# A selective scan in pairs: one scan instruction over two units, with ScalarE writing the restart of the second

## The reference, cut to what matters

```
x_dbl = einsum('bkdl,kcd->bkcl', xs, x_proj_weight)      # dt (6), B (16), C (16)
delta = softplus(dt_proj(dt) + bias)                     # 96 channels
h     = exp(delta * A) * h + (delta * u) * B             # 16 states for each channel, over l
y     = sum over the states of h * C, + D * u
```

## Time and profile before

| What | us |
|---|---|
| median of 3 runs | 5436.18 |
| lowest, highest | 5427.06, 5442.36 |
| span of the profiled execution | 5432.0 |
| VectorE busy in it | 4515.3 |
| GpSimd busy | 4129.8 |
| TensorE busy | 4644.7 |
| ScalarE busy | 2890.6 |

### The profile page before, as it was taken

How to read it: one execution, slowest core, us unless ns; L and a number is a source line. 1 busy time by engine, 2 the same in 40 slices (tenths; PEclk the granted TensorE clock), 3 DMA queues, 4 the chain that set the end, 5 groups by cost and what they waited for, 6 DMA issues and landing times. The chain is left out here.

```text
span 5432.0 us, 72922 instructions
## 1 busy us (share of the span) xinstructions
PE 4644.7 (86%) x15210; PEld 2119.9 (39%) x15210; DVE 4515.3 (83%) x4928; ACT 2890.6 (53%) x4502; POOL 4129.8 (76%) x2854
## 2 busy tenths in 40 slices
PE   7998887956999999963978888888888888888887
PEld 2332554623666666642522222222222222222222
DVE  4776445452599999997969999999999999999996
ACT  6885555621111111111357767777777777777776
POOL 2454545532589898987869999999999999999993
PEclk9998999978999999986989999999999999999998
DMA  2000101067677777744057667666776776677773
GB/s 52 1 1 14 56 22 51 27 191 208 130 146 146 143 146 142 149 85 99 0 142 188 185 186 189 184 185 189 187 189 179 188 189 187 181 188 188 187 186 94
DMA packets 385402, 733.35 MB, mean 135 GB/s; under 512 B 77948, under 2 KB 119080, under 8 KB 370920
## 3 DMA queue, kind: packets, MB, share of 16 engines
q1 hardware_dynamic: 385128, 730.30, 54.8%
HBM read 594.31 MB, written 82.32 MB: 125 GB/s over the span
## 5 line engine op out<-in xcount | busy, mean ns | idle before, releaser
L2194 POOL TENSOR_TENSOR l_hc<-l_h,l_c_rep 128x512 f32<-128x512 f32 x1536 | 1927.8, 1273 | 211.3 <-DVE l_h L2248 181.1
L2248 DVE TENSOR_TENSOR_SCAN l_h<-l_p_da,l_h,l_bu 128x512 f32<-128x512 f32 x1120 | 1403.4, 1269 | 5.0 <-ACT l_p_da L2099 2.5
L2099 ACT ACTIVATE l_p_da<-l_p_da,l_a_neg 128x512 f32<-128x512 f32 x1536 | 1008.1, 657 | 729.3 <-PE l_p_da L1954 713.1
L1400 POOL TENSOR_TENSOR l2b_prod<-l2b_v,l2b_attn 128x1568 f32<-128x1568 f32 x276 | 937.3, 3449 | 232.1 <-ACT l2b_attn L1361 116.7
L1954 PE MATMUL l_p_da<-l_stacked,l_pick 96*128 96x512 f32 x1536 | 908.4, 593 | 190.3 <-DVE l_h L2248 180.5
L2233 DVE TENSOR_TENSOR l_bu<-l_du_rep,l_p_b 128x512 f32<-128x512 f32 x1280 | 840.8, 657 | 27.9 <-DMA l_du_rep<-du_scratch 22.2
L1954 PEld LDWEIGHTS l_p_da<-l_stacked,l_pick 96*128 96x128 f32 x1536 | 293.2, 192 | 1161.0 <-DVE l_h L2248 896.8
L1448 DVE TENSOR_REDUCE l2b_osum<-l2b_prod 128x32 f32<-128x1568 f32 x384 | 665.7, 1780 | 63.0 <-POOL l2b_prod L1400 59.3
L1962 PE MATMUL l_p_y<-l_hc,l_y_pick 128*32 128x512 f32 x3072 | 562.9, 626 | 71.8 <-POOL l_hc L2194 71.7
L1353 ACT ACTIVATE l2b_logits<-l2b_conv,l2b_this_b 98x512 f32<-98x512 f32 x96 | 66.2, 689 | 861.5 <-PE l2b_conv L1318 861.5
L1318 PE MATMUL l2b_conv<-l2b_img_high,l2b_w_conv_high 128*98 128x512 f32 x1344 | 356.2, 418 | 32.2 <-DMA l2b_img_low<-qkv_scratch 32.2
(11 more groups left out here) (261 smaller groups left out, 8495.8 us busy)
## 6 DMA issues: line engine op xcount, KB each, us to landing
l_du_rep<-du_scratch SPq DMA_DIRECT2D x1536, 256.0 KB, 3.8
l2b_img_high<-qkv_scratch SPq DMA_DIRECT2D x192, 306.2 KB, 5.7
l2b_img_low<-qkv_scratch SPq DMA_DIRECT2D x192, 306.2 KB, 9.5
l_stacked<-l_parts SPq DMA_DIRECT2D x512, 96.0 KB, 2.7
l2b_v<-v_scratch SPq DMA_DIRECT2D x192, 152.0 KB, 6.5
qkv_scratch<-l2a_strip SPq DMA_DIRECT2D x32, 840.0 KB, 5.2
du_scratch<-l_du SPq DMA_DIRECT2D x128, 192.0 KB, 2.1
l_w_raw<-L_w_sed SPq DMA_DIRECT2D x32, 576.0 KB, 3.7
```

The source lines that it names most:

```text
L1400: return eng.tensor_tensor(dst.rearrange("q x (dy dx) -> q x dy dx", dx=WIN), window, attn_half[:, :, unit % 2].rearrange("q x (dy dx) -> ...
L2099: act.activation(p_da[i % DAS][:], p_da[i % DAS][:], ACT.Exp, scale=a_neg[:, k * G + GRP[i]:k * G + GRP[i] + 1]).then_inc(s_da, 1)
L2194: pool.tensor_tensor(hc[:, (G * par + i) % HCS, :], h[:, i, :], c_rep[:, par, :], ALU.mult).then_inc(s_hc, 1)
L2248: dve.tensor_tensor_scan(h[:, i, way], p_da[i % DAS][:, way], of, state, ALU.mult, ALU.add).then_inc(s_h, 1)
```

## The change

The 12 units become 6 pairs. One scan instruction now covers two units, 128x1024, over one flat row of 1024 columns. For the second unit to begin afresh, its decay in the first column is set to 0 and its own beginning, old decay x last h + bu, is written into `bu`. ScalarE does this (`decays`): it saves the exponential of that column (`joint_da`), does the two exponentials of 511 and 512 columns, writes the 0 into PSUM and writes the new `bu` column, with scale and bias from columns. Backward directions scan the flat row from its end, so there it is unit 0 of the pair that is restarted. `p_da` is now two pairs of banks, and `p_y` one bank for two.

The products by B and by C are made in pairs too: VectorE has four B pairs (0, 1, 3, 4), GpSimd two (2, 5), where VectorE had ten units and GpSimd two. du is made by VectorE, straight from the PSUM bank. `kept` is gone; delta's constant comes in by a 97th row of the operands. SyncE stores du ahead of the restack. TensorE, ScalarE and GpSimd have new orders.

```diff
             def decays(n, k, c, p):
+                act.wait_ge(s_rep, G * n + 2 * p + 1)
+                act.activation(joint_da[:, p % 2:p % 2 + 1], da[:, e, at:at + 1], ACT.Exp, scale=rate(2 * p + e)).then_inc(s_join, 1)
+                act.activation(da[:, e, rest], da[:, e, rest], ACT.Exp, scale=rate(2 * p + e))
+                act.wait_ge(s_rep, G * n + 2 * p + 2)
+                act.activation(da[:, 1 - e, :], da[:, 1 - e, :], ACT.Exp, scale=rate(2 * p + 1 - e))
+                act.wait_ge(s_join, PAIRS * n + p + 1)
+                cut = act.activation(da[:, e, at:at + 1], zero[:], ACT.Copy)
...
+                    act.activation(of, joint_da[:, p % 2:p % 2 + 1], ACT.Identity, bias=of, scale=before).then_inc(s_da, 1)
...
             def delta_u(m, b, k, c):          # now on VectorE
+                dve.wait_ge(s_hi, m + 1 + HI0)
+                dve.wait_ge(s_dus, 16 * m + DUS0)
+                dve.tensor_tensor(du[:], p_bc[0:C, :], u_of(b, k, c), ALU.mult).then_inc(s_du, 1)
...
             def low_mm(m):
-                pe.wait_ge(s_hi, m + 1 + HI0)
+                pe.wait_ge(s_du, m + 1 + DU0)
...
             def step(b, n, k, c, par, n1, n2, before):      # VectorE
+                times_b(n, 1, par)
+                scan(n, k, c, 0, par)
+                scan(n, k, c, 1, par)
+                if n1:
...
+                    delta_u(n + 1, *n1)
+                times_b(n, 3, par)
+                scan(n, k, c, 2, par)
+                times_b(n, 4, par)
+                scan(n, k, c, 3, par)
+                scan(n, k, c, 4, par)
+                if n1:
+                    times_b(n + 1, 0, 1 - par)
+                scan(n, k, c, 5, par)
...
             def step(b, n, k, c, par, n1, n2, before):      # GpSimd
+                if before:
+                    times_c(n - 1, 5, 1 - par)
+                times_b(n, 2, par)
+                times_c(n, 0, par)
+                times_c(n, 1, par)
+                times_c(n, 2, par)
+                times_b(n, 5, par)
+                times_c(n, 3, par)
+                times_c(n, 4, par)
...
             def step(b, n, k, c, par, n1, n2, before):      # ScalarE
+                c_copy(n, par)
+                decays(n, k, c, 0)
+                if n1:
+                    log_1e(n + 1)
+                decays(n, k, c, 1)
+                if n1:
+                    delta_and_high(n + 1, 1 - par)
+                decays(n, k, c, 2)
+                if before:
+                    take_y(n - 1, *before)
+                if n1:
+                    low(n + 1)
+                decays(n, k, c, 3)
+                if n1:
+                    b_copy(n + 1, 1 - par)
+                if k == 0:
...
+                        turn_x(b, c + 2)
...
+                decays(n, k, c, 4)
+                if n2:
+                    abs_relu(n + 2, n2[1])
+                    exp_x(n + 2)
+                decays(n, k, c, 5)
+                if n2:
+                    one_plus(n + 2)
```

More of the change, by code:

```diff
@@ L1709, in selective_scan @@
     TRIPLES = G // YT
-    HCS = 8
-    DAS = 3
-    BUS = 3
+    LAST_PAIR = [(YT * t + YT - 1) // 2 for t in range(TRIPLES)]
+    HCP = 4
     RING = 8
-    ON_POOL = (5, 11)
-    BU_AHEAD = 4
-    NB = G - len(ON_POOL)
+    POOL_PAIRS = (2, 5)
+    DVE_PAIRS = tuple(p for p in range(PAIRS) if p not in POOL_PAIRS)
+    NB, NP = len(DVE_PAIRS), len(POOL_PAIRS)
     COLS = N // H
@@ L1830, in ring_count, with hc_at, joint, first_column @@
             return 16 * (G // 4 * (n - par) // (RING // 4) + (G * par + i) // RING) + 16
-        def vector_bus(i):
-            return sum(j not in ON_POOL for j in range(i))
+        def hc_at(par, p):
+            return 2 * ((PAIRS * par + p) % HCP)
+        def joint(k):
+            return 1 if k < 2 else 0
+        def first_column(k):
+            return 0 if k < 2 else N - 1
+        def end_column(k):
+            return N - 1 if k < 2 else 0
         def stacked_by(m, par):
@@ L1923, in c_mm @@
                     pe.nop(nofuse=True)
-                pe.matmul(p_bc[:], w_rep[:, k, 1, :], u_of(b, k, c), start=True, stop=True).then_inc(s_c, 1)
+                pe.matmul(p_bc, w_rep[:, k, 1, :], u_of(b, k, c), start=True, stop=True).then_inc(s_c, 1)
             def b_mm(m, par, b, k, c):
@@ L2106, in take_y @@
                 if k in (0, 2):
-                    act.activation(y_sum[:, bass.ds(at * N, N)], p_y[par][:], ACT.Copy).then_inc(s_y, 1)
+                    act.activation(y_sum[:, bass.ds(at * N, N)], p_y, ACT.Copy).then_inc(s_y, 1)
                 else:
@@ L2151, in _ @@
+                if k == 0 and isinstance(c, int) and c < 2:
+                    turn_x(b, 2 * c + 1)
             for m in range(2):
@@ L2250, in step, with delta_u @@
-            def step(b, n, k, c, par, n1, n2, before):
-                for i in range(G):
-                    if i < G - 1 and i + 1 not in ON_POOL:
-                        times_b(n, i + 1, par)
-                    if i == G - 1 and n1:
-                        times_b(n + 1, 0, 1 - par)
-                    scan(n, k, c, i, par)
+            def delta_u(m, b, k, c):
+                dve.wait_ge(s_hi, m + 1 + HI0)
+                dve.wait_ge(s_dus, 16 * m + DUS0)
+                dve.tensor_tensor(du[:], p_bc[0:C, :], u_of(b, k, c), ALU.mult).then_inc(s_du, 1)
```

414 lines of the change are left out of this document (195 added, 219 removed).

## The result

| | median of runs, us | profiled execution, span, us |
|---|---|---|
| before | 5432.67 | 5432.0 |
| changed | 5445.05 (5420.53 to 5458.66) | 5456.5 |

Both medians are of 20 runs; the profiled one of the changed kernel is the slowest of its 20, 14 us above the median. The ratio to before is 1.0023, with a 95% interval of 1.0014 to 1.0032: slower by 12 us, where 98 us less were forecast. The forecast was 5335, its range 5245 to 5430. The change does nearly nothing to the time, and the question is where 1.4 us of VectorE's work a step went.

The account below looks back on a forecast made before the run. VectorE was taken to bound the kernel at 20.12 us a step; afterwards the chain through low and SyncE would set 19.3. 5432 - 105 + 3 = 5330 for the profile, 5335 for the median, range 5245 to 5430.

Parts of the forecast that it names:

- VectorE: VectorE after the change: 6 scans, 4 products and one du, 18.7 us a step (18.6 to 19.5), 1.4 us gained.
- the bare rival: du_rep lands in time or TensorE is quicker, so VectorE's own 18.7 us is the step: 5256 us; chance 0.25.
- GpSimd: GpSimd does 16 halves in 8 instructions of 2.34 us: 18.7 us a step, as full as VectorE but with slack.
- ScalarE's block D: ScalarE's work for a pair, two exponentials and three one-column activations: about 1.65 us, ends 1.5 and 2.3.
- Fine at 1.65: Between scans p-2 and p, ScalarE's block for a pair has some 2.85 us, so its 1.65 us fits.
- The chain through `low` and SyncE: du, low_mm, low, restack, du_rep: landing at 15.5 or 16.3 us makes steps of 18.9 or 19.7, mean 19.3; chance 0.43.
- turn_x at nothing: ScalarE's 1.1 us turn_x could delay pair 4's block, 32 times, 35 us at most; taken as zero.
- No wait of scans for the restart: ScalarE, 16.3 us a step, was not to delay scans; the rival that its restart does: about 5600 us, chance 0.14.
- the forecast's own sign that it is wrong: The forecast called itself wrong if scans wait for ScalarE, or if GpSimd or VectorE has no idle time.
- the case that had 0.08: Something smaller or mixed, in no one named place, leaves the time as it is; chance 0.08.
- lie beside this: Matmuls of decays, the C and B projections and ScalarE's logs were put off the deciding chain, with no time added.

Follow-up runs that it names:

- both orders: Against the changed kernel: first two du_rep ahead of the restack, low_mm ahead of y_whole, low and pair 3's exponentials ahead of take_y; 5298.13 us (0.974).

## Why the prediction was wrong

Its own steps, in its order:

- **VectorE: right.** Bare 18.6 us, forecast 18.7. A merged scan takes 2.255 (2.28), a product 1.12 (1.12), du 0.58 (0.58). The saving on VectorE, 1.5 us a step, is really there, and 5263.5 us with the waits out of the way stands close to the 5256 of the bare rival.
- **GpSimd: right.** 2.33 us a pair from start to start, forecast 2.34:

```profile
3901.64 2.37 POOL L2208 TENSOR_TENSOR l_hc<-l_h,l_c_rep 128x1024 f32<-128x1024 f32 x1 [0.44 <-DVE l_h L2279]
3903.97 2.37 POOL L2197 TENSOR_TENSOR l_pool_bu<-l_du_rep,l_b_sb 128x1024 f32<-128x1024 f32 x1
3906.30 7.12 POOL L2208 TENSOR_TENSOR l_hc<-l_h,l_c_rep 128x1024 f32<-128x1024 f32 x3
```

  It is never the bound while the waits are there, and as full as VectorE once they are gone (491.21 and 490.29 of 500).
- **ScalarE's block D: right in size,** 1.65 us as forecast: 0.14, two of 0.57, 0.09, 0.28. The three small ones are 0.51 of it, 3.1 us a step, as the rows had given. But a right size was not enough for "Fine at 1.65": what stands ahead of a block counts as well (below). With TensorE's gap filled, the 18 instructions cost 97 us.
- **The chain through `low` and SyncE: right in kind, 0.4 us short** in a steady step. Counted from the next product's start, as the forecast counts, the product that needs `du_rep` comes at 15.9 us in steps with the straight copy (forecast 15.5) and at 16.8 in the others (16.3): a steady step is 19.3 and 20.2, mean 19.75, where 18.9 and 19.7 stood. Some 0.25 us of it lie up to the restack's issue, 0.2 from there to the product (7.4 for 7.2), where the second du_rep lands 3.85 us after its issue and not 3.5. 128 x 0.45 is 58 us.
- **turn_x at nothing: wrong, the step that failed most clearly.** "I take zero, since 0.8 us of slack and the du wait absorb it" is false. The 24 steps average 21.08 us in the changed kernel, 1.6 above the 19.45 that their steady kinds would give: 39 us. Some 11 of them are the change of image, which stays when `turn_x` has moved; the other 28 are within the 35 that I had as the most. Halving the copy gives 25 us back, and moving it 35 on top of both orders. The du wait does not absorb it: in those 24 steps the DMA wait is 5 us in all, the wait for ScalarE 37, of it 17 at scan 4. The one wait takes the other's place, and more.
- **No wait of scans for the restart: wrong.** This was the forecast's own sign that it is wrong. 71 us, or 80 with the waits for the other results of the block. Some 37 lie in the steps of turn_x and 16 in the second step of each later k (twelve steps). Some 20 lie in the 52 other steps with the strided `take_y` (0.38 each): it was forecast as TensorE's time alone, while ScalarE's copy of 1.07 us also stands ahead of pair 3's block. The rest is scattered.
- **TensorE's clock: not foreseen.** In the second step of k = 1, 2 and 3 (the third column of the table, twelve steps in all) TensorE waits 1.4 to 1.8 us ahead of replicate 1, and in nine of them it then runs at 1.2 GHz for a while:

```profile
3921.04 0.73 PE L1964 MATMUL l_p<-l_stacked,l_pick 96*128 96x512 f32 x2 [1.74 <-DVE l_h L2279]
3921.61 1.02 PE L1952 MATMUL l_p<-l_log_e,l_plus 96*96 96x512 f32 x2
3922.47 1.72 PE L1953 MATMUL l_p<-l_relu_x,l_plus 97*96 97x512 f32 x2
3924.12 1.93 PE L1973 MATMUL l_p<-l_hc,l_y_pick 128*32 128x512 f32 x6
3925.98 0.76 PE L1964 MATMUL l_p<-l_stacked,l_pick 96*128 96x512 f32 x2
```

  Replicate 2 comes 5.0 us after scan 5's end, where the step before has 3.4, and `low` ends at 10.8 for the 9.1 forecast. Scan 3 then waits 1.65 us, as shown above. The three of the twelve whose matmuls stay at 593 ns are the comparison: their replicate 2 comes at 3.4, and their entries in the step table are 19.9, 20.1 and 20.2, while the nine have 21.2 to 23.1, 21.85 in the mean. That makes some 18 us. With the other late steps outside `turn_x` it is some 37 us (102 steps of 20.18 in the mean, where steady ones of their kinds would be 19.8); for those other late steps no run shows a cause.

58 + 39 + 37 = 134 us against the 20.31 - 19.3 = 1.0 us, 129 in all, that the sum missed. This is bookkeeping of one profile and not three experiments. `turn_x` was tried by itself. The clock's effect is shown where the restart is left out, 121 us, and in the changed kernel by the nine steps beside the three; the filling could not show it there, since it lengthened the path. Why the gap becomes 1.7 us just there stays open. So does what lets the clock fall: of 18 idle stretches of 1.4 us or more ahead of replicate 1 in the changed kernel (the last step aside), 11 are followed by the low clock and 7, of up to 2.00 us, are not.

The chances were off in kind as well. The chain was the likeliest case, and its terms but one, the landing of du_rep, were within 0.25 us of what steady steps show. What came is the case that had 0.08, something mixed that leaves the time as it is. A mean over steps was made from steady steps alone, and every term that was left at nothing ("lie beside this", "absorb it") had the same sign. Once VectorE had 1.4 us less to do a step and the chain took that place, nothing was left to absorb anything: the first rival of such a sum is that several small ones add up.

## What to carry to other kernels

When the bounding engine gets faster, the work behind it in program order turns from cover into path: list for each producer (here SyncE's queue and ScalarE) what stands ahead of the item that the fast engine needs, and move that behind it. Here three moves of a few lines, du_rep ahead of the restack, `low` ahead of the y work, `turn_x` into an idle gap, turned 0.2% slower into 3.1% faster than before. And read a loop step by step before a mean is trusted: the irregular steps held more than half of the loss here (39 + 37 of 134 us). A filler for an idle gap must be shorter than the gap in every step; here each was longer than the mean gap, and it cost over half of what it takes. And a run that leaves work out can be slower for another reason, here the clock: look at that first, before the work is called free.

## What the runs showed of the hardware

- A VectorE product with both inputs in SBUF waited for the GpSimd products that ran: 4.80 us in place of 0.66, 3.3 in the mean. The GpSimd products were hardly slowed (2405 ns for 2364).
- A scan of 1024 columns takes 2.255 us from start to start, chained, against 2 x 1.20 for two of 512; the merge saves 0.15 us. The three one-column activations last 0.19, 0.27 and 0.40 us in the mean, with 0.09, 0.14 and 0.28 from start to start.
- Behind an idle stretch of TensorE, 1.74 and 2.10 us in the rows shown, matmuls ran at the lower clock: 1057 ns for 593. Not each such stretch did this: in the changed kernel 7 of 18 between 1.4 and 2.1 us did not. Where 81 of 128 steps had the slow matmuls, filling the gap gave back 121 us, the filler's own cost included.
